# A fused attention and state-space block in fp32: a polynomial's multiply moved from VectorE to GpSimd, one first product moved the other way, and the tile loops written out

## What is computed

```
x = x + attention(group_norm(x))            # 4x4 blocks, pooled
x = x + mamba(layer_norm(group_norm(x)))    # projected, layer-normed again
```

```
dt = softplus(dt @ dt_proj.T + dt_b)
A = -exp(A_log)
for every position t and each of the 16 states s:
    h[s] = exp(dt * A[s]) * h[s] + (dt * xc) * B[s]
    y    = sum over s of h[s] * C[s]
y = (y + xc * D) * silu(z);  y = y @ out_proj.T
```

## Time and profile before

| | |
|---|---|
| median of 3 runs | 16619.03 us (16615.55 to 16625.17) |
| the profiled execution | 16605.28 us |
| its span, first to last instruction | 16603.5 us |
| mean granted TensorE clock | 0.941 of 2.4 GHz |
| VectorE busy | 91% |
| GpSimd busy | 90% |
| TensorE matmul busy | 87% |
| ScalarE busy | 68% |

### The profile page before, as it was taken

One profiled execution on the slowest core, in us unless ns is written; L12 is line 12 of the kernel. 1 busy time (PEld: TensorE's weight loads), 2 busy tenths in 40 slices (PEclk: granted clock), 3 DMA queues, 4 the chain that ended last, 5 costly groups with the idle time before them and its releaser, 6 DMA issues. The chain is left out here.

```text
span 16603.5 us, 158027 instructions
## 1 busy us (share of the span) xinstructions
PE 14390.7 (87%) x30720; PEld 5782.7 (35%) x30720; DVE 15104.1 (91%) x13023; ACT 11266.2 (68%) x18635; POOL 15002.7 (90%) x6275
## 2 busy tenths in 40 slices
PE   6888888888888888888888888888888888888888
PEld 2333333333333333333333333333333333333333
DVE  6999999999999999999999999999999999998988
ACT  5666667666666666666677666667666676667675
POOL 5999889998899989998899998999989999899998
PEclk9999999999999999999999999999999999999999
DMA  3444444444444444444444444444444444444443
GB/s 132 155 154 161 150 152 154 155 157 150 154 154 153 163 145 153 156 154 159 142 155 160 152 160 143 156 156 158 155 143 156 156 157 158 146 148 158 150 151 135
DMA packets 738975, 2535.44 MB, mean 153 GB/s; under 512 B 77240, under 2 KB 78016, under 8 KB 721728
## 3 DMA queue, kind: packets, MB, share of 16 engines
q1 hardware_dynamic: 738112, 2527.45, 44.8%
HBM read 2376.15 MB, written 150.99 MB: 152 GB/s over the span
## 5 line engine op out<-in xcount | busy, mean ns | idle before, releaser
L1467 POOL TENSOR_TENSOR RING<-RING,CS 128x1024 f32<-128x1024 f32 x4096 | 9833.9, 2416 | 1369.6 <-DVE RING L1148 1350.2
L1148 DVE TENSOR_TENSOR_SCAN RING<-DA,HS,RING 128x512 f32<-128x512 f32 x8192 | 9955.4, 1264 | 811.0 <-ACT DA L777 614.1
L388 PE MATMUL YP<-RING,EYE 128*128 128x512 f32 x16384 | 8293.4, 638 | 1648.6 <-POOL RING L1467 1578.7
L777 ACT ACTIVATE DA<-ITEM,AN 128x512 f32<-128x512 f32 x8192 | 5519.4, 685 | 3384.9 <-DVE RING L1148 3376.5
L388 PEld LDWEIGHTS YP<-RING,EYE 128*128 128x128 f32 x16384 | 3133.4, 199 | 6324.9 <-issue 3616.5
L1128 DVE TENSOR_TENSOR RING<-DTP,BS 128x1024 f32<-128x1024 f32 x2816 | 3375.5, 1206 | 0.4 <-DMA BS<-bc_rows 0.3
L1454 POOL TENSOR_TENSOR RING<-ITEM,BS 128x1024 f32<-128x1024 f32 x1280 | 3016.6, 2357 | 9.4
L388 PE MATMUL FL<-XN,WC 128*128 128x512 f32 x4096 | 1943.3, 618 | 9.7 <-ACT XN L864 4.6
L388 PEld LDWEIGHTS FL<-XN,WC 128*128 128x128 f32 x4096 | 839.4, 205 | 1129.8 <-issue 1121.5
L791 ACT ACTIVATE ITEM<-FL,COL 128x512 f32<-128x512 f32 x512 | 347.6, 679 | 1183.1 <-PE FL L388 1183.1
L388 PE MATMUL FL<-LS,WP 128*128 128x512 f32 x2048 | 995.6, 610 | 35.3 <-DVE XR L1184 29.2
(11 more groups left out here) (123 smaller groups left out, 10636.4 us busy)
## 6 DMA issues: line engine op xcount, KB each, us to landing
BS<-bc_rows SPq DMA_DIRECT2D x2048, 512.0 KB, 4.9
CS<-bc_rows SPq DMA_DIRECT2D x2048, 512.0 KB, 3.6
XR<-in_x SPq DMA_DIRECT2D x128, 1024.0 KB, 7.3
x_slices<-XR SPq DMA_DIRECT2D x64, 1024.0 KB, 8.1
XR<-x_slices SPq DMA_DIRECT2D x64, 1024.0 KB, 7.5
out<-XR SPq DMA_DIRECT2D x64, 1024.0 KB, 8.2
XR<-in_wqkv SPq DMA_DIRECT2D x24, 1024.0 KB, 7.3
bc_rows<-ROWS SPq DMA_DIRECT2D x256, 64.0 KB, 4.6
```

The lines of the kernel that those rows point to most:

```text
L388: return pe.matmul(*a, **k)
L777: act.activation(DA[:, h, :], DT[:, i % 2, h, :], ACT.Exp, scale=AN[:, h, s:s + 1]).then_inc(dA_ready, 1)
L1148: dve.tensor_tensor_scan(H[:, slot(n), h, :], DA[:, h, :], U[:, slot(n), h, :], HS[:, i % ITEMS, h, s:s + 1], ALU.mult, ALU.add).then_inc( ...
L1467: pool.tensor_tensor(G[:, slot(n)], H[:, slot(n)], CS[:, s % C_ROWS, :].unsqueeze(1).broadcast_to([P, NH, T]), ALU.mult).then_inc(g_ready, 1)
```

## The change

Three things are changed.

1. The polynomial's constant is added by ScalarE: a second activation (Identity with a bias column, in place on YZ) stands right behind the square. The multiply by EM is a plain tensor_tensor of GpSimd, in step 10 (11 where d = 1), after the last product of that step and before `dt_sum`. VectorE has no part in it.
2. VectorE makes the first product of state 8 (in step 6, before scan 6), so that it makes twelve and GpSimd four.
3. The inner loops over tiles are written out on all engines; the outer loop over images stays.

```
-POOL_U = (0, 1, 2, 7, 8)
+POOL_U = (0, 1, 2, 7)
-AHEAD = ((), (), (3,), (4, 5), (6,), (), (), (9,), (10,), (11,), (12,), (13,), (14,), (15,), (), ())
+AHEAD = ((), (), (3,), (4, 5,), (6,), (), (8,), (9,), (10,), (11,), (12,), (13,), (14,), (15,), (), ())
...
                 act.activation(YZ[:, :, :], EM[:, :, :], ACT.Square, bias=CUBE_SHIFT, scale=CUBE).then_inc(square_ready, 1)
+                act.wait_ge(square_ready, tile * ITEMS + i + 1)
+                act.activation(YZ[:, :, :], YZ[:, :, :], ACT.Identity, bias=CUBE_REST).then_inc(factor_ready, 1)
...
-            def dt_poly(tile, i):
-
-                dve.wait_ge(square_ready, tile * ITEMS + i + 1)
-                dve.scalar_tensor_tensor(out=YZ[:, :, :], in0=YZ[:, :, :], scalar=13.0 / 16, in1=EM[:, :, :],
-                                         op0=ALU.add, op1=ALU.mult).then_inc(poly_ready, 1)
...
-                    if front:
-                        if s == 10 + d:
-                            dt_poly(tile, w + 1)
...
+            def dt_poly(tile, i):
+                pool.wait_ge(factor_ready, tile * ITEMS + i + 1)
+                pool.tensor_tensor(YZ[:, :, :], YZ[:, :, :], EM[:, :, :], ALU.mult).then_inc(poly_ready, 1)
...
                         if s == 10 + d:
+                            dt_poly(tile, w + 1)
                             dt_sum(tile, w + 1)
...
-                with dve.Fori(0, 4) as t:
+                for t in range(4):
                     for w in range(2, 2 + ITEMS):
                         window(b * NT + t, w, stat=(b + 1, t) if w == 3 else None)
-                with dve.Fori(4, 6) as t:
+                for t in range(4, 6):
```

More of the change, by code:

```diff
@@ L102, in block_ssm_kernel @@
         AN = sb("AN", [P, NH, NS])
-        COL = sb("COL", [P, 46])
+        COL = sb("COL", [P, 47])
         SM = sb("SM", [P, 88])
@@ L111, in block_ssm_kernel @@
         SKIP, EPSC, BV16, PBF = COL[:, 30:31], COL[:, 31:32], COL[:, 32:36], COL[:, 36:40]
-        NSMALL, ONESMALL, CUBE_SHIFT, ZERO, NLOGSMALL, LOGSMALL = (COL[:, n:n + 1] for n in range(40, 46))
+        NSMALL, ONESMALL, CUBE_SHIFT, ZERO, NLOGSMALL, LOGSMALL, CUBE_REST = (COL[:, n:n + 1] for n in range(40, 47))
         Q, K = QK[:, 0], QK[:, 1]
@@ L327, in image @@
                 tile_step(b, 0, tile, after_store=(b - 1, NT - 1) if b else None, stats=early(0))
-                with sp.Fori(1, 4) as t:
+                for t in range(1, 4):
                     tile_step(b, t, tile + t, after_store=(b, t - 1), stats=early(t))
-                with sp.Fori(4, 6) as t:
+                for t in range(4, 6):
                     tile_step(b, t, tile + t, after_store=(b, t - 1), stats=pair(t))
@@ L750, in _ @@
             with pe.Fori(0, BATCH - 1) as b:
-                with pe.Fori(0, NT - 2) as t:
+                for t in range(NT - 2):
                     for w in range(2, 2 + ITEMS):
@@ L759, in _ @@
             b = BATCH - 1
-            with pe.Fori(0, NT - 1) as t:
+            for t in range(NT - 1):
                 for w in range(2, 2 + ITEMS):
@@ L1083, in _ @@
             act.activation(AN[:, :, :], AN[:, :, :], ACT.Exp).then_inc(an_exp, 1)
-            act.wait_ge(mean_ready, 8)
+            act.wait_ge(mean_ready, 9)
             act.activation(NLOGSMALL, ZERO, ACT.Ln, bias=ONESMALL).then_inc(logsmall_ready, 1)
@@ L1094, in _ @@
             with act.Fori(0, BATCH - 1) as b:
-                with act.Fori(0, NT - 2) as t:
+                for t in range(NT - 2):
                     for w in range(2, 2 + ITEMS):
@@ L1106, in _ @@
             b = BATCH - 1
-            with act.Fori(0, NT - 1) as t:
+            for t in range(NT - 1):
                 for w in range(2, 2 + ITEMS):
@@ L1373, in first_front @@
                 scale_norm(tile + 1)
-                dt_poly(tile, 0)
                 dve.wait_ge(state_zeroed, image + 1)
@@ L1401, in _ @@
             dve.memset(CUBE_SHIFT, -0.75 * CUBE).then_inc(mean_ready, 1)
+            dve.memset(CUBE_REST, 13.0 / 16).then_inc(mean_ready, 1)
             dve.tensor_scalar(BV16, BV, float(SS), None, ALU.mult).then_inc(mean_ready, 1)
@@ L1434, in _ @@
             b = BATCH - 1
-            with dve.Fori(0, NT - 1) as t:
+            for t in range(NT - 1):
                 for w in range(2, 2 + ITEMS):
@@ L1516, in _ @@
             dt_first(0, 0)
+            dt_poly(0, 0)
             dt_sum(0, 0)
@@ L1524, in _ @@
             with pool.Fori(0, BATCH - 1) as b:
-                with pool.Fori(0, NT - 1) as t:
+                for t in range(NT - 1):
                     for w in range(2, 2 + ITEMS):
```

6 lines of the change are left out of this document (3 added, 3 removed).

## The result

The changed kernel takes 17027.12 us (median of 4 runs, 17018.98 to 17046.25); the kernel before, timed beside it, 16621.56 us (4 runs, 16615.55 to 16625.17). The ratio is 1.0247, with a 95% interval of 1.0235 to 1.0260. The forecast was 17107 us, with a range of 16840 to 17260.

What follows compares the result with a forecast made beforehand. A ring of mutual waits through VectorE, GpSimd and TensorE was taken as the bound. 387 + 81 + 30 - 10 = +488 us on the profiled 16605.3 gave 17093, plus 14 to the median: 17107 us, range 16840 to 17260.

Steps and rivals of the forecast that it cites:

- The ring: Loop of mutual waits: VectorE from gate to scan 10, GpSimd through product 14, TensorE to the next gate; 61.48 us.
- tail: GpSimd's part of the ring behind product 10, through product 14; the ring's whole GpSimd stretch is 21.78 us.
- (a): The polynomial leaves VectorE, 539 us in all, but stands behind scan 10, hidden by the tail: direct gain 0.
- (b): GpSimd's product 10 is no longer slowed by VectorE's polynomial running beside it: gain 0.95 us an item.
- (c): The multiply enters GpSimd's tail between product 10 and dt_sum: cost 2.31 us an item, bounds 0 and 2.42.
- (d): State 8's first product leaves GpSimd ahead of product 10, where GpSimd already idles up to scan 10: gain 0.
- (e): VectorE makes state 8's first product between gate and scan 10: cost 1.12 us an item, 0.3 where j = 2.
- (f): ScalarE's added activation in step 10 is wanted only after product 10: cost 0, at most 1.13 us an item.
- (g): Written-out loops remove 41 jumps; counted only in an image's sixth tile, where the gate doesn't wait: gain 10 us.
- TensorE's clock: Rivals on TensorE's low clock before the gate: at nearly every gate, 17227 us (0.14); vanished, 16971 us (0.11).
- full items: Some 50 items near the first seven images' ends, VectorE alone the path: +0.6 us each, between -0.98 and +2.48.
- normal items: Some 156 items, all j = 0, j = 1 and 3 except in last tiles: +2.48 us each.

## Why the prediction was right

Direction and mechanism hold, and the size is 80 us too large (17107 for 17027); between the traces the forecast was +488 for a measured +441. Some of that closeness is luck: the single kinds of window missed by up to 1.6 us, and the misses cancel.

- **The ring bounds the kernel.** Shown three times for the normal tiles: a product moved from a 90% busy GpSimd to VectorE makes the kernel slower (state 8 alone, +189), it lengthens the way from gate to scan 10 by 1.14 to 1.37 us, and a shorter tail shortens the kernel (one operand from PSUM, -349).
- **The ring's path.** The prediction followed one window with j = 0 and took the others to be like it. It named as a sign of being wrong that product 10 starts well after scan 10 ends, and for j = 1 and 2 it does, by about 1.2 us, because VectorE hands over at scan 9 there. It also said that both engines idle in every item, and for j = 1 GpSimd is idle for only 0.16 us between the products 3 and 10. The sum doesn't suffer, since state 8's product stands ahead of both scans and the multiply behind both.
- **(a) the polynomial's own time, 0** where the tail covers it. Whether it is covered in the full tiles is open; see the last point of this list.
- **(b) lock, -0.95 an item.** Confirmed: product 10 takes 2.35 us, and without the lock the tail is 0.88 us shorter.
- **(c) multiply, +2.31.** It measured 2.50: the multiply itself takes its 2.36, but `dt_sum` starts 0.14 us after that has ended, since it waits for its own engine's result (36.7 us of idle time over 256, 0.14 each). (b) and (c) together were +1.36; the tail grew by 1.46 to 1.58.
- **(d) state 8 off GpSimd, 0.** Right in the change alone by the sum, wrong as a rule: with the multiply in the tail, GpSimd has no time left ahead of product 9 where j = 1, and the move then gives back part of what it costs. The two parts are 98 us cheaper together than apart. In the full windows it is likely not 0 either (last point).
- **(e) state 8 on VectorE, +1.12.** Measured 1.13, 1.13 and 1.37 for j = 0, 1 and 3. For j = 2 the whole window grew by 1.32 where the prediction had 1.66; there the way to scan 10 became shorter by 0.9, which I had not foreseen. In those windows of the kernel before VectorE waits 1.82 us for ScalarE's decays between gate and scan 10, and in the changed kernel not at all. The new product fills part of that wait; the rest goes with the multiply, for with the multiply alone 1.05 us are left of it.
- **(f) activation, 0.** It ends before product 10 starts; by itself 36 us in all, with VectorE's polynomial still behind it.
- **(g) loops, -10.** 32 us alone, nothing to be seen within the change, where 10 could not be told from nothing.
- **TensorE's clock.** Neither rival came. The low clock changed places: the gates that end j = 0 windows, which had it before, now seldom do, and those that end j = 1 windows do. Counted from the end of product 14 to the gate, the granted clock is below 0.95 in 52 of 63 windows with j = 0 before and in 6 after, in 12 and 54 of 64 with j = 1, and in 136 and 122 of all. What moves it is open. This is the sum of state 14 at the end of the next window (j = 1), the row that took 1.98 us above:

```profile
2928.58 3.28 PE L388 MATMUL YP<-RING,EYE 128*128 128x512 f32 x4 [2.09 <-POOL RING L1460]
```

  In the table j = 0 wins 1.39 us from product 14 to the gate and j = 1 loses 1.51. That is why the window with j = 0 grew by 1.31 and that with j = 1 by 4.06, though both were forecast at 2.48. A normal tile was forecast at 3 x 2.48 + 1.66 = 9.10 us and measured 8.93; that the two kinds of window cancel is the luck spoken of above.
- **The step that missed: the 50 full items at +0.6.** The three last tiles of an image were to grow by 15.8 us (by the same count four normal items, one with j = 2 and seven full ones at 0.6), and they grew by 7.5. That is 8.3 x 7 = 58 us, more than the whole overshoot of 47. I took the middle of -0.98 and +2.48. Window by window, the seven shrink by 2.0 us in all, -0.3 each, and the other five grow by 9.6 where 11.6 were forecast. The reason that the prediction gave, that VectorE is the path alone there, was read from one window (j = 2, the second full tile), which has the most to do and shrinks by 2.4 us. In the other six VectorE is idle for 2.5 to 14.6 us in the kernel before, and with state 8 alone, which only adds to VectorE, the seven become 2.9 us shorter, where VectorE alone as the path would make them 7 x 1.12 = 7.8 longer. So they gain elsewhere, most likely from the relief of GpSimd, which (d) had at 0; which wait gives it back is open.

Of the signs that I named: GpSimd's wait for scans was to be about 2100 us and is 1973, the busy shares 87% and 86% and are 87% and 87%, product 10 to product 14 was to be 20.8 us and is 20.98, and the gate still waits (515 us, 497 before). Two waits grew more than any other and were not in the forecast: ScalarE's for `dt_x` and VectorE's for ScalarE. The second lies behind scan 10: between gate and scan 10 of a normal tile's four windows VectorE waits 2.0 us for decays, where it was 3.6. That both follow from the longer tail is the likely reading; no run tests it.

## What to carry to other kernels

When two engines are both about 90% busy and still wait for each other in every round, follow one round from a wait back to the same wait, and cost an edit by whether it stands on that ring: an operation taken from the slack gives nothing as long as slack is left, and one put between the handoffs costs its full length, unless it fills a wait. Follow a round of every kind: here the handoff stood one step earlier in half of them. Moving work from one engine to the other is then no trade, even where both end up less busy, as here. Parts that each use the same slack must also be run together, since 189 and 314 us alone were 405 in one kernel.

## What was unexpected of the hardware

- The lock between VectorE and GpSimd falls on either side. With two operands in SBUF the polynomial averages 2105 ns against 1197 with one in PSUM, and beside a GpSimd that does not pause it took 6.26 us, while three GpSimd operations ran one behind another. Where GpSimd was the one held, it lost 0.9 us.
- An operation that needs the result of the one right ahead of it on the same engine starts late: 0.28 us on VectorE (a first product, then its scan), 0.14 on GpSimd (the multiply, then `dt_sum`).
- An idle 1.11 us of VectorE and 1.95 us of ScalarE at one jump of a loop: writing out 41 of them was worth 32 us in one kernel and nothing that can be measured in the other.
